# Two attention layers in one kernel: the value products of the first layer move into the middle of the next step, a repeated score product goes, and the second layer's sums are copied a little earlier

## What is computed

```python
# first layer: 8 heads, each a mixture of 2 softmaxes over 784 pooled keys
attn = softmax(einsum('bnd,bdk->bnk', q, k2) / 4)         # n = 3136, k = 784, d = 8
attn = (attn * pi).sum over the 2 parts                    # pi from the mean query
x = conv1x1(einsum('bnk,bvk->bnv', attn, vt), w_out) * inv * gamma + beta + x
# second layer: LayerNorm over channels, 8 heads of 16, 3136 keys, and a learned position bias
sim = einsum('bhdi,bhdj->bhij', q, k) / 4 + bias
x = conv1x1(softmax(sim) @ v, w_out) + x
```

## Time and profile before

| | us |
|---|---|
| three runs | 3760.82, 3760.30, 3749.16; median 3760.3 |
| the profiled execution | 3773.08, its span 3771.3 |
| mean granted PE clock over the span | 0.938 |
| PE busy | 3555.4 (94%) |
| DVE busy | 2797.6 (74%) |
| ACT busy | 2315.8 (61%) |
| POOL busy | 849.0 (23%) |

### The profile page before, as it was taken

How to read it: one execution, slowest core, us unless ns; L and a number is a source line. 1 busy time by engine, 2 the same in 40 slices (tenths; PEclk the granted TensorE clock), 3 DMA queues, 4 the chain that set the end, 5 groups by cost and what they waited for, 6 DMA issues and landing times.

```text
span 3771.3 us, 70851 instructions
## 1 busy us (share of the span) xinstructions
PE 3555.4 (94%) x27690; PEld 1087.8 (29%) x27690; DVE 2797.6 (74%) x8284; ACT 2315.8 (61%) x2830; POOL 849.0 (23%) x935
## 2 busy tenths in 40 slices
PE   6998998999998899999999999999999999999997
PEld 2222222222222223333333223333333333333332
DVE  5567767777776678877887777788887788888870
ACT  2566657666668436666666666656666656666665
POOL 2144334333432512022111012210102211100000
PEclk6789889988889869999999999999999999999999
DMA  1188887600000312332233222223322233233221
GB/s 54 15 54 55 57 53 57 48 16 17 21 12 13 78 39 78 84 88 70 71 83 96 73 73 73 74 74 92 89 74 70 76 89 79 73 89 87 77 59 28
DMA packets 268053, 236.35 MB, mean 63 GB/s; under 512 B 222184, under 2 KB 225112, under 8 KB 267464
## 3 DMA queue, kind: packets, MB, share of 16 engines
q1 hardware_dynamic: 241544, 205.85, 29.0%
q0 software_dynamic: 26176, 25.98, 3.3%
HBM read 226.65 MB, written 27.19 MB: 67 GB/s over the span
## 4 chain that ended last, share of the span: by engine, by line
PE 80%; DVE 9%; issue 7%; ACT 2%; POOL 1%; DMA 1%; POOLq 0%; SPq 0%; ACTq 0%; DVEq 0%
PE P L731 26%; PE P L716 16%; PE P L684 11%; PE P L697 9%; DVE maxes L1051 7%; PE P L673 5%; PE P L757 5%; PE P L807 2%; PE P L701 2%; PE P L784 1%; ACT probs L940 1%; PE P L773 1%; PE P L819 1%; ACT L989 0%; POOL high L539 0%
## 5 line engine op out<-in xcount | busy, mean ns | idle before, releaser
L940 ACT ACTIVATE probs<-P 128x896 f32<-128x896 f32 (+1 forms) x2352 | 2044.3, 915 | 1265.2 <-PE P L716 872.7
L1070 DVE CUSTOM_DVE_ANT_0 junk<-P,mstage 112x448 bf16<-112x448 f32 x3136 | 1830.0, 622 | 460.0 <-PE P L684 455.3
L731 PE MATMUL P<-probs,vals 128*17 128x448 f32 (+1 forms) x9408 | 1181.8, 576 | 23.4 <-ACT sums L1016 22.8
L1051 DVE TENSOR_REDUCE maxes<-P 128x1 f32<-128x392 f32 (+1 forms) x1600 | 796.4, 558 | 336.8 <-PE P L673 336.0
L716 PE MATMUL P<-bstage,flip 112*56 112x448 f16 x6272 | 740.6, 358 | 0.0
L684 PE MATMUL P<-keys,q_stack 48*112 48x448 f16 x3136 | 622.9, 380 | 4.1 <-DVE maxes L1070 3.9
L697 PE MATMUL P<-q_two,keys 49*128 49x448 f16 x3136 | 560.9, 355 | 15.3 <-ACT probs L940 15.3
L673 PE MATMUL P<-keys,q_stack 24*128 24x392 f16 (+1 forms) x1600 | 415.2, 367 | 84.7 <-DVE maxes L1051 52.3
L539 POOL TENSOR_SCALAR high<-projected,cst 128x448 f16<-128x448 f32 x112 | 157.0, 1402 | 1247.4 <-ACT projected L949 1203.0
L716 PEld LDWEIGHTS P<-bstage,flip 112*56 112x56 f16 x6272 | 277.4, 106 | 351.2 <-issue 226.8
L697 PEld LDWEIGHTS P<-q_two,keys 49*128 49x128 f16 x3136 | 150.8, 93 | 716.3 <-ACT probs L940 645.1
(11 more groups left out here) (129 smaller groups left out, 1440.3 us busy)
## 6 DMA issues: line engine op xcount, KB each, us to landing
mstage<-g_max SPq DMA_DIRECT2D x56, 1519.0 KB, 8.0
bstage<-g_bias SPq DMA_DIRECT2D x28, 1568.0 KB, 8.1
bstage<-g_bias SPq DMA_DIRECT2D x28, 1519.0 KB, 8.6
g_max<-t_bf SPq DMA_DIRECT2D x16, 673.8 KB
keys<-d_rden POOLq DMA_DIRECT2D x42, 224.0 KB, 6.1
rwide<-d_rden POOLq DMA_DIRECT2D x42, 224.0 KB, 4.7
g_bias<-t_hi SPq DMA_DIRECT2D x8, 679.9 KB
g_bias<-t_lo SPq DMA_DIRECT2D x8, 679.9 KB
```

Source lines behind the costliest of these rows:

```text
L731: last = mm(P[32 * h:32 * h + HD + 1, PV, 0:QB], table[0:kr, kt, h, :], probs[0:kr, s % 3, h, :], start=kt == 0, stop=kt == unit.tiles - 1 ...
L940: A(probs[0:kr, s % 3, 2 * p:2 * p + 2, :], P[0:kr, 2 * p:2 * p + 2, 0:QB], ACT.Exp).then_inc(exp_done, 1)
L1051: V.tensor_reduce(out=maxes0[0:size, unit.i % 2, t, HALVES[r], c:c + 1], in_=P[0:size, bank_of(job), 0:HALF], op=ALU.max, axis=AX.X).then_ ...
L1070: V.tensor_tensor_reduce(out=junk[:, PLAN.nth[job] % 4, :], in0=P[0:QT, bank_of(job), 0:QB], in1=bias, scale=1.0, scalar=-3.0e38, op0=ALU. ...
```

## The change

In the first layer `values(s - 2)` stands in the middle of step s, between r1 and r2, in place of `values(s - 1)` at the end of it. The repeated scores of half 1 are made once. In the second layer `values(s - 1)` stays at the end of the step; its first two steps take over the two value products that the first layer has left. On ACT, in the second layer, the copy of the sums stands ahead of the step's first exponential; before, it stood between the two.

```diff
-            def scores(s, p, final=True):
+            def scores(s, p):
...
-                if not unit.biased and final:
+                if not unit.biased:
                     last.then_inc(st_made, 1)
...
             for s in range(-PRE, LAST + POST):
                 if 0 <= s < LAST and STEPS[s][0].biased:
+                    if s - 2 < BASE[FIRST1]:
+                        values(s - 2)
                     scores(s, 0)
...
                     beside(s, "b")
+                    if s - 1 >= BASE[FIRST1]:
+                        values(s - 1)
                 else:
                     inside, groups = 0 <= s < LAST, [g for w in "ab" for g in PLAN.pairs[s, w]]
...
                     if inside:
                         scores(s, 0)
-                    for g in groups[:1]:
-                        if not g[0].biased:
-                            first_pass0(*g, 1)
-                            first_pass0(*g, 2)
+                    for g in own:
+                        first_pass0(*g, 1)
+                    if inside and s >= 2:
+                        values(s - 2)
+                    for g in own:
+                        first_pass0(*g, 2)
                     if inside:
-                        scores(s, 1, False)
                         scores(s, 1)
...
-                if 1 <= s <= LAST:
-                    values(s - 1)
+                    if s == LAST:
+                        values(s - 1)
...
             for s in range(-PRE, LAST + POST):
                 for p, w in enumerate("ab"):
-                    if 0 <= s < LAST:
+                    sums_first = 0 <= s < LAST and STEPS[s][0].biased
+                    if 0 <= s < LAST and not sums_first:
                         exponentials(s, p)
                     for j in at_stage("copied", s) if p == 0 else []:
...
                         A(sums_of(j), P[:, PV, 0:QB], ACT.Copy).then_inc(sums_made, 1)
+                    if sums_first:
+                        exponentials(s, p)
                     beside(s, w)
```

More of the change, by code:

```diff
@@ L888, in _ @@
                     beside(s, "b")
+                    if s - 1 >= BASE[FIRST1]:
+                        values(s - 1)
                 else:
                     inside, groups = 0 <= s < LAST, [g for w in "ab" for g in PLAN.pairs[s, w]]
-                    for g in groups[:1]:
-                        if g[0].biased:
-                            first_pass1(*g)
-                        else:
-                            first_pass0(*g, 0)
+                    own = groups[:1] if groups and not groups[0][0].biased else []
+                    for g in groups[:1 - len(own)]:
+                        first_pass1(*g)
+                    for g in own:
+                        first_pass0(*g, 0)
                     if inside:
                         scores(s, 0)
-                    for g in groups[:1]:
-                        if not g[0].biased:
-                            first_pass0(*g, 1)
-                            first_pass0(*g, 2)
+                    for g in own:
+                        first_pass0(*g, 1)
+                    if inside and s >= 2:
+                        values(s - 2)
+                    for g in own:
+                        first_pass0(*g, 2)
                     if inside:
-                        scores(s, 1, False)
                         scores(s, 1)
-                    for g in groups[:1]:
-                        if not g[0].biased:
-                            first_pass0(*g, 3)
+                    for g in own:
+                        first_pass0(*g, 3)
                     for g in groups[1:]:
```

## The result

| | before | after |
|---|---|---|
| median of four runs, us | 3754.7 | 3644.6 |
| lowest to highest | 3741.7 to 3760.8 | 3627.7 to 3669.5 |
| ratio | | 0.972, 95% interval 0.968 to 0.976 |
| profiled execution, its span | 3773.1, 3771.3 | 3630.8, 3629.0 |
| mean granted clock over the span | 0.938 | 0.952 |

The account below looks back on a forecast made before the run. It took a ring of waits to bound the first layer and PE alone the second. 3773 - 73 - 23 + 34 = 3711 us for the profiled execution, so a median of 3698; range 3625 to 3790.

Parts of the forecast that it names:

- The ring of the plain step: First-layer steps without a job: a chain of waits between PE and DVE keeps them at 2.14 us, gain nothing.
- Steps with a job: First layer: query projection 3.36 to 2.67 us, output projection 3.35 to 2.83, turn of maxima 2.91 to 3.10.
- the first layer's -73: Gain in the first layer: -48 us from 56 units and -25 from other jobs; bounds 0 and -107.
- roughly 50 other jobs: First-layer steps with bias network, key projections or some moments: 50 x 0.5 = -25 us.
- The turn's cost: First-layer step with the turn of the maxima: next scores wait for ACT's later shift, +0.19 us at 2.4 GHz.
- The sums: Second layer: PE's values no longer wait for ACT's copy of the sums, -23 us, bounds -25 and -8.
- The clock: First layer: fewer scores mean eight points more time at 1.2 GHz, +34 us, bounds -20 and +130.
- a clock over 0.92: Granted clock from 300 us to the first layer's end: near 0.84 expected; over 0.92 would show the prediction wrong.
- rival B: First layer: without the repeated products the clock falls in plain stretches, loss 125 to 167 us, 3789 to 3831, chance 0.17.
- D: First layer: steps tighten and a denser PE keeps its clock or gains, 3590 to 3660 us, chance 0.20.
- A: Steps as laid out, clock from slightly better to 16 points worse: 3660 to 3735 us, chance 0.50.
- C: Steps with jobs gain little as ACT's or DVE's work fills the hole, only sums won: 3735 to 3750, chance 0.13.

Follow-up runs that it names:

- the 37: 37 more runs of the unchanged kernel before, made beside the experiments; clocks of 0.930 to 0.956, 3598 to 3609 us at full clock.
- halves, both earlier: Changed kernel with values made in two halves of 224 columns, and the maxima's turn and queries' projection one step earlier: 3621.5 us, ratio 0.962.
- before - repeats: Kernel before with only the repeated score products taken out, values still at the end of the step: 3883.4 us, ratio 1.039.
- turn earlier: Changed kernel with the first layer's products for the maxima and their turn one step earlier: 3698.5 us, ratio 0.985.

## Why the prediction was right, and where it was wrong

**The ring of the plain step: right.** 2.14 us at clock 1.00 with 0.15 idle, as before; at 0.50 3.23 (3.22 before).

**Steps with a job: right.** Medians at clock 1.00: projection of queries 2.61 (forecast 2.67), output projection 2.61 (2.83), turn 3.14 (3.10). The output step was mis-sized because DVE's addition pushes nothing. In one of after it starts at 298.00 us and takes 0.68, the reductions follow at 298.60 with no idle time, and from values to values the step is 298.34 - 295.73 = 2.61, as long as the projection step, which has no addition. At clock 0.50 steps with a projection last 4.53 (4.7) where they took 5.11, the turn step 4.38 for 4.19.

That the first layer's -73 came as -71 at full clock is in part luck, since two errors cancel. A unit gained 2 x 0.75 - 0.23 = 1.27 us at clock 1.00, where 1.02 had been put, and 0.97 at clock 0.50, where 0.4 had been put. At full clock the 52 units of the 364 steps make 52 x 1.27 = 66 of the 71 us. So the roughly 50 other jobs, put at 25 us, brought about 5.

The turn's cost was named with its cause, r1 behind the scores behind ACT's shift; that this stand is also where the clock gives way was not.

**The sums: right.** -23 forecast; -24 to -25 in the changed kernel's second layer. The kernel with this edit alone is 31 us faster in the medians, of which 26 are length at full clock.

**The clock: wrong.** This is the step that failed: "I take eight points more time at 1.2 GHz", a loss of 34 us. In the profiled pair the share at clock 0.50 went the other way, from 334/1167 = 29% to 202/1049 = 19%. Over all runs it did not change by anything that can be told: 397 and 390 us at clock 0.50, a gain of 3 us. By the prediction's own sign, a clock over 0.92 from 300 us on meant that it was wrong; it was 0.93 in the profiled run. The account of the 53 us between 3698 and 3644.6 is then: 6 us because the median of before came out lower, 7 because the kernel got 103 us shorter at full clock where 96 had been put, and some 40 for the clock: the 34 of loss did not come, and the four runs of before in the result were a little slower than most of the 37.

The working took one fall and asked only what the removed products had done for the stretch ahead of it. In the old order that was right, and more so than the prediction said: alone, their removal costs 137 us, with some 150 us of clock lost and a little length won. That is rival B's own size (125 to 167). But the new order does not need them, and they would cost 74 us there. An effect of one part, argued in the old order, was carried over to the new one. No row and no run shows the eight points; they were the author's estimate, and this fall was thin ground for it: 2.94 of 3.40 us busy is 86%, and the 98.9 us at clock 1.00 ahead of it were 89% busy.

**That fall was not a typical one.** It comes where a set of seven units, which share one group of keys, ends. There one step holds two groups of products for the maxima; PE makes five of them in a row, each waiting for DVE to free its bank, and nothing else for over 2 us. The kernel before at its fall of 805.8 us, and the changed kernel at its fall of 726.4:

```profile
804.95 2.39 PE L673 MATMUL P<-keys,q_stack 24*128 24x392 f16 x5 [0.27 <-DVE maxes L1051]
```

```profile
723.40 3.87 DVE L1059 TENSOR_REDUCE maxes<-P 128x1 f32<-128x392 f32 x8
...
724.02 2.23 PE L673 MATMUL P<-keys,q_stack 24*128 24x392 f16 x5
```

Between 300 and 1050 us such a row of five comes at clock 1.00 five times in the kernel before and six times in the changed one. The clock fell all eleven times, during the row or at most 1.9 us behind it. The kernel before has its repeats there and the changed one does not, and both fall. So the fall that the prediction took as its example does not turn on the repeats.

**The rivals.** The time lies in D's range (3590 to 3660) and 15 us outside A's (3660 to 3735), though what happened is mostly A: the plain steps are as A laid them out and the others nearly so, and the clock is unchanged, inside A's condition. A's sum without the 34 us would have been 3664. That the time fell into the stated range is owed to the range's width. B's mechanism is real and did not occur in this combination. C is refuted: jobs no longer stretch their step by 1.2 but by 0.5 us.

**Open.** Why the old order needs the repeats and the new one does not is not settled. In the profiled run the changed kernel holds clock 1.00 for 113 to 119 us at a time four times. Of its seven falls between 300 and 1000 us, six are those at the ends of sets (340.7, 473.9, 600.2, 726.4, 859.6 and 989.3 us, some 126 to 133 us apart), and only one, at 900.5, is elsewhere; the kernel before has others between the sets. The 0.60 us lull comes in every unit and mostly passes. That the new order moves each job between two sets of values fits, but no run shows it alone. No run spreads the five products at the end of a set either, which would test what those falls cost.

## What to carry to other kernels

Cost an edit that touches PE in two terms, its length at full clock and the time at clock 0.50, and expect the second to depend on the combination: products that hold the clock up in one order can pull it down in another (in the old order 807 us at 0.50 without the repeats for 397 with them, in the new one 390 for 509), so they are tried again after every reordering. Take both terms from several runs: one profiled pair showed 48 us of clock here where the medians show 3. Before reasoning from one fall of the clock, look at whether the others come in the same place. When a job is moved earlier to close a hole, move what feeds it as well; a hole that only changes its owner may cost more, as the 1.69 us for 0.60 did. And the forecast of step lengths from one ring of waits, read off a timeline, was good at clock 1.00 to 0.06 us for three kinds of step; the fourth was 0.22 off. The larger doubt belongs to the clock.

## What the runs showed of the hardware

- A busy PE is not a PE at full clock. The clock fell behind 3.40 us in which PE was busy for 3.40 (halves, both earlier), with its products for the maxima half as wide as usual. It stood at clock 0.50 for 122.9 us with PE busy 115.29 (before - repeats). The changed kernel held clock 1.00 for 119.5 us with PE busy 107.13, only 90%.
- The falls have places. At the row of five products for the maxima at the end of a set the clock fell 11 times out of 11, in the kernels before and after.
- A lull much shorter than a step matters. The clock fell at or within 4 us behind 7 of 48 stands in the changed kernel (most of 0.60 us), 13 of 45 with the repeats (0.72) and 21 of 27 with the turn earlier (1.4 in the mean). Stands are not the whole of it: the fall behind 3.40 busy us, and the 26 of 31 falls of the kernel before with no stand of 0.5 us ahead, came without one.
- With a stand of 1.67 us once a unit the kernel fell into a rhythm, 3.4 us at clock 1.00 and 23.9 at 0.50; together 27.3, which is about the length of a unit at 0.50 (27.0 by the prediction's estimate), and it often repeated. That kernel spent 1187 us of one layer at clock 0.50 and is 9.7% slower than the kernel before.
- Executions of one and the same kernel differ in this: the changed kernel's four runs spread over 42 us with clocks from 0.937 to 0.952, and 0.015 x 2 x 3650 x 0.36 = 39 us of it are clock. Their lengths at full clock agree within 3 us.
